# A chunked state-space stage whose front moves into the previous chunk's scan loop, with one more quarter of the summing on GpSimd for every second state

## The reference

```python
proj = einsum('blh,eh->ble', hidden, in_proj_w)
x, gate = proj[..., :1024], proj[..., 1024:]
u = silu(causal_conv4(x, conv_w) + conv_b)
dt_lr, Bm, Cm = split(einsum('bld,rd->blr', u, x_proj_w))       # 128 + 16 + 16
delta = softplus(einsum('blr,dr->bld', dt_lr, dt_proj_w) + dt_proj_b)
A = -exp(A_log)
h = h * exp(delta_t * A) + (delta_t * u_t) * B_t                 # 16 states for each of 1024 channels
y_t = sum over n of h[.., n] * C_t[n]
y = (y + u * D) * silu(gate)
out = einsum('bld,hd->blh', y, out_proj_w)
```

## Time and profile before

| | |
|---|---|
| median of 3 runs | 3812.79 us (3812.38 to 3813.08) |
| the profiled execution, its time | 3813.42 us |
| its span | 3811.6 us |
| PE, DVE, ACT, POOL busy in the span | 3318.6, 3286.4, 2489.4, 2454.7 us |
| mean granted TensorE clock | 0.942 |
| HBM traffic | 40 GB/s over the span |

### The profile page before, as it was taken

One profiled execution on the slowest core, in us unless ns is written; L12 is line 12 of the kernel. 1 busy time (PEld: TensorE's weight loads), 2 busy tenths in 40 slices (PEclk: granted clock), 3 DMA queues, 4 the chain that ended last, 5 costly groups with the idle time before them and its releaser, 6 DMA issues.

```text
span 3811.6 us, 46308 instructions
## 1 busy us (share of the span) xinstructions
PE 3318.6 (87%) x12672; PEld 2365.7 (62%) x12672; DVE 3286.4 (86%) x6128; ACT 2489.4 (65%) x4790; POOL 2454.7 (64%) x1943
## 2 busy tenths in 40 slices
PE   5888984999999999999999999999999999985738
PEld 4666662666767676767676767666666666663515
DVE  5888883299999998989898989898989898989891
ACT  4777672186767676767676858676767676765650
POOL 0344343086869595959595959595969595957470
PEclk8999997999999999999999999999999999987868
DMA  2222212111111111111111111111111111101010
GB/s 99 65 74 73 76 61 84 61 37 40 30 43 31 42 33 41 39 34 41 34 41 34 41 33 41 34 39 35 40 35 39 35 39 37 47 27 37 20 36 6
DMA packets 119378, 165.36 MB, mean 43 GB/s; under 512 B 8545, under 2 KB 84193, under 8 KB 118625
## 3 DMA queue, kind: packets, MB, share of 16 engines
q1 hardware_dynamic: 119136, 162.63, 15.2%
HBM read 128.39 MB, written 25.69 MB: 40 GB/s over the span
## 4 chain that ended last, share of the span: by engine, by line
POOL 28%; PE 20%; DVE 17%; issue 15%; ACT 2%; DVEq 1%; POOLq 0%; DMA 0%; SPq 0%; ACTq 0%
POOL dBu L866 16%; POOL yacc L879 12%; DVE D L1308 10%; PE W L1064 6%; PE W L1114 5%; PE W L1096 3%; PE W L1137 2%; DVE prod L1327 2%; PE W L1141 2%; DVE D L1330 2%; PE D L1064 1%; DVE U L1259 1%; DVE yacc L1339 1%; ACT L916 1%; DVE hT L1221 1%
## 5 line engine op out<-in xcount | busy, mean ns | idle before, releaser
L1308 DVE TENSOR_TENSOR_SCAN D<-D,hc,dBu 128x256 f32<-128x256 f32 x2048 | 1436.9, 740 | 47.0 <-ACT D L1007 47.0
L866 POOL TENSOR_TENSOR dBu<-U,BC 128x512 f32<-128x512 f32 x1024 | 1294.3, 1275 | 276.4 <-DMA BC<-bc_scratch 200.3
L1064 PE MATMUL W<-nT,wffn 128*128 128x256 f32 x5632 | 1241.6, 382 | 47.2 <-ACT nT L905 32.6
L1064 PEld LDWEIGHTS W<-nT,wffn 128*128 128x128 f32 x5632 | 1058.8, 189 | 230.6 <-ACT nT L905 37.5
L1007 ACT ACTIVATE D<-delta,A 128x256 f32<-128x256 f32 x2048 | 891.7, 468 | 425.7 <-DVE yacc L1339 404.8
L879 POOL TENSOR_TENSOR yacc<-yacc,prod 128x512 f32<-128x512 f32 x736 | 933.9, 1269 | 263.0 <-DVE prod L1327 258.5
L1096 PE MATMUL W<-wffn,hT 128*128 128x512 f32 (+1 forms) x1408 | 642.0, 613 | 41.5 <-DVE hT L1221 41.5
L1096 PEld LDWEIGHTS W<-wffn,hT 128*128 128x128 f32 (+1 forms) x1408 | 273.8, 197 | 373.4 <-issue 323.8
L1327 DVE TENSOR_TENSOR prod<-D,BC 128x512 f32<-128x512 f32 x736 | 494.6, 672 | 0.0
L1064 PE MATMUL W<-nT,win 128*128 128x256 f32 x2048 | 453.9, 383 | 33.7 <-ACT nT L905 33.7
L1064 PEld LDWEIGHTS W<-nT,win 128*128 128x128 f32 x2048 | 391.4, 192 | 106.4 <-ACT nT L905 44.9
(11 more groups left out here) (118 smaller groups left out, 3212.0 us busy)
## 6 DMA issues: line engine op xcount, KB each, us to landing
BC<-bc_scratch SPq DMA_DIRECT2D x256, 256.0 KB, 4.6
XM<-x_scratch SPq DMA_DIRECT2D x29, 512.0 KB, 4.9
X<-x_scratch SPq DMA_DIRECT2D x17, 512.0 KB, 3.6
ix<-idx SPq DMA_DIRECT2D x33, 255.0 KB, 2.9
X<-x SPq DMA_DIRECT2D x16, 512.0 KB, 3.4
XR<-x SPq DMA_DIRECT2D x16, 512.0 KB, 3.4
x_scratch<-XR SPq DMA_DIRECT2D x16, 512.0 KB, 3.7
out<-X SPq DMA_DIRECT2D x16, 512.0 KB, 2.8
```

The lines of the kernel that those rows point to most:

```text
L866: nc.gpsimd.tensor_tensor(dBu[e % 4][:], U[:, 2 * j:2 * j + 2, :], BC[slot][:, 0:1, :].to_broadcast([P, 2, CH]), ALU.mult).then_inc(s_dBu, 1)
L1064: last = T_.matmul(dst, lhsT, rhs, start=(n == 0), stop=(n == len(terms) - 1))
L1308: V.tensor_tensor_scan(D[:, m, :], D[:, m, :], dBu[e % 4][:, m % 2, :], hc[:, n, m:m + 1], ALU.mult, ALU.add).then_inc(s_scan, 1)
```

## The change

The front of chunk k = i + 1 is worked off within step i. Its first product stands on TensorE right behind the gate half of chunk i; its taps, convolution and Silu stand at fixed elements of loop i on ScalarE and VectorE; its low-rank and B/C products stand inside the late `ffn`, between the two downward products (`x_proj`), and its delta product (`delta_proj`) behind that `ffn`, one pair of D at a time as loop i gives it up. below, soft and to_delta of the pairs 0 to 2 run over the end of loop i, those of pair 3 over the end and the first element of loop i + 1. For this U * delta goes to a tile of its own (dU) and nT is double; the convolution reads W in PSUM directly (no xext), and the three columns at its edge are formed by GpSimd (`edges`) from a tile `tail` and added by VectorE (`ends`). The output projection stands undivided behind the first half of the gate product, its residual is added in two halves. XM keeps a chunk from the first gated layer to its norm for the state-space layer, so x2 isn't loaded back for that. The hand-placed table load (L960) is gone. The rescale of hc by keep becomes one memset at the start of the second sequence. Steps are written out for every chunk, with constants instead of registers. GpSimd's `add` takes pair 3 too where the state is even, in all chunks. `places` (the steady case is quoted) has all element numbers; the scratch for dynamic DMA is set to 4096.

```diff
+        def by_pool(e):
+
+            return e % 4 < 3 or e % 8 == 3
+
+        def upto(e):
+
+            return sum(by_pool(u) for u in range(e))
...
+                return dict(stat=stat, early=(1, 3), late=(8, 10), m=(NEVER, NEVER), m2=(41, 43), out=(4, 6),
+                            norm=5, gate=(9, 12), evac=18, silu=(21, 24, 27, 29, 32, 34), res=38,
+                            norm2=36, evac2=39, silu2=(44, 46, 49, 52, 54, 56), res2=NEVER, norm_m=NEVER, evac_m=NEVER, norm_m2=58, evac_m2=NEVER,
+                            taps=(14, 17), conv=(12, 14), smooth=(21, 21, 24, 24), low=61, bc=63)
...
+                def edges(k):
+
+                    pool.wait_ge(m_tail, 2 * k + 2)
+                    pool.wait_ge(m_edge, 2 * k)
+                    nc.gpsimd.tensor_tensor(edge[:], tail[:], cw[:, :, 0:1].to_broadcast([P, ME, KC - 1]), ALU.mult).then_inc(m_term, 1)
+                    for d in (1, 2):
+                        pool.wait_ge(m_term, 5 * k + 2 * d - 1)
+                        w = KC - 1 - d
+                        nc.gpsimd.tensor_tensor(term[:, :, 0:w], tail[:, :, d:KC - 1], cw[:, :, d:d + 1].to_broadcast([P, ME, w]),
+                                                ALU.mult).then_inc(m_term, 1)
+                        pool.wait_ge(m_term, 5 * k + 2 * d)
+                        nc.gpsimd.tensor_tensor(edge[:, :, 0:w], edge[:, :, 0:w], term[:, :, 0:w], ALU.add).then_inc(m_term, 1)
...
-                    N_.preload_act_table_set("natural_log_exp_and_others")
...
+                def taps(k, q):
+
+                    act.wait_ge(m_x, 2 * k + q // 2 + 1)
+                    act.wait_ge(m_du, 4 * k)
+                    for h in range(2):
+                        m = 2 * q + h
+                        N_.activation(U[:, m, :], W[q // 2][:, m % 4, :], ACT.Identity, bias=cb[:, m:m + 1],
+                                      scale=cw[:, m, KC - 1:KC]).then_inc(m_tap, 1)
+
+                def smooth(k, q):
+
+                    act.wait_ge(m_edge, 2 * k + q // 2 + 1)
+                    N_.activation(U[:, 2 * q:2 * q + 2, :], U[:, 2 * q:2 * q + 2, :], ACT.Silu).then_inc(m_u, 1)
...
+                def soft(k, j):
+
+                    act.wait_ge(m_below, 4 * k + j + 1)
+                    N_.activation(dBu[j][:], dBu[j][:], ACT.Exp).then_inc(m_exp, 1)
+                    act.wait_ge(m_exp, 4 * k + j + 1)
+                    N_.activation(dBu[j][:], dBu[j][:], ACT.Ln, bias=1.0).then_inc(m_ln, 1)
...
+                        if e == 0:
+                            soft(i, 3)
+                        if e < 4:
+                            skip(i, e)
+                        if f1 and e == at["norm"]:
+                            norm(norm_no(*early(i)), early_rows, ffn_no(*early(i)))
...
+                            if i + 1 < NC and e == at["taps"][h]:
+                                taps(i + 1, 2 * h)
+                                taps(i + 1, 2 * h + 1)
+                        if f1 and e == at["evac"]:
+                            evac(norm_no(*early(i)), i % 2, 0)
...
+                        if i + 1 < NC and e == at["low"]:
+                            low_rank(i + 1, 1 - side_late(i))
+                        if i + 1 < NC and e == at["bc"]:
+                            b_and_c(i + 1, 1 - side_late(i))
+                    if 0 < i < NC - 2:
+                        evac(norm_no("M", i + 2), i % 2, 0)
+                    for j in range(4):
+                        save(i, NE - 4 + j)
+                        if i + 1 < NC and j < 3:
+                            soft(i + 1, j)
...
+                def x_proj(k, side):
+
+                    pe.wait_ge(m_u, 4 * (k + 1))
+                    dt = chain(W[side][:, 0, :], [(wx[:, m, 0:R], U[:, m, :]) for m in range(ME)])
+                    dt.then_inc(m_dt, 1)
+                    bc = chain(W[side][0:2 * S, 2, :], [(wx[:, m, R:R + 2 * S], U[:, m, :]) for m in range(ME)])
+                    bc.then_inc(m_bc, 1)
+
+                def delta_proj(k):
+
+                    pe.wait_ge(m_dtl, k + 1)
+                    for j in range(4):
+                        if k:
+                            e = NE - 4 + j
+                            pe.wait_ge(s_prod, NE * (k - 1) + e + 1)
+                            pe.wait_ge(s_ha, pool_sums(k - 1) + upto(e + 1))
+                        for m in (2 * j, 2 * j + 1):
+                            last = T_.matmul(D[:, m, :], wdt[:, m * P:(m + 1) * P], dtl[:], start=True, stop=True)
+                        last.then_inc(m_dp, 1)
...
                     down(0, MI - 1)
+                    if low is not None:
+                        x_proj(low, 1 - side)
                     for k in range(MI):
                         if k == TURN_AT and then is not None:
+                            if low is not None:
+                                pe.wait_ge(m_bcS, low + 1)
                             turn(then, 1 - side)
                         last = down(1, k)
...
+                def step(i):
+
+                    done_norms = norm_no(*early(i)) if i + 2 < NC else norm_no(*late(i))
+                    done_ffns = ffn_no(*early(i)) if i + 2 < NC else ffn_no(*late(i))
+                    pe.wait_ge(n_T, done_norms)
+                    pe.wait_ge(f_res, done_ffns)
                     pe.wait_ge(m_bcS, i + 1)
-                    for h in range(2):
...
+                    for m in range(4):
+                        last = gate(i, m)
+                    last.then_inc(m_g, 1)
+                    if i:
+                        project(i - 1)
+                    for m in range(4, ME):
+                        if i and m % 2 == 0:
+                            pe.wait_ge(m_res, 2 * (i - 1) + m // 2 - 1)
+                        last = gate(i, m)
+                    last.then_inc(m_g, 1)
+                    L, F = norm_no(*late(i)), ffn_no(*late(i))
...
+                        first(i + 1, 0)
+                        pe.wait_ge(m_sg, 2 * i + 2)
+                        first(i + 1, 1)
+                        pe.wait_ge(m_tail, 2 * i + 5)
+                        free = (m_tail, 2 * i + 6)
...
+                def conv(k, q):
+
+                    dve.wait_ge(m_tap, ME * k + 2 * q + 2)
...
+                            if d:
+                                dve.wait_ge(m_conv, 24 * k + 6 * q + 2 * (d - 1) + h + 1)
+                            V.scalar_tensor_tensor(U[:, m, KC - 1 - d:CH], W[q // 2][:, m % 4, 0:CH - KC + 1 + d], cw[:, m, d:d + 1],
+                                                   U[:, m, KC - 1 - d:CH], ALU.mult, ALU.add).then_inc(m_conv, 1)
...
+                def ends(k, h):
+
+                    half = slice(4 * h, 4 * h + 4)
+                    dve.wait_ge(m_term, 5 * (k + 1))
+                    V.tensor_scalar(tail[:, half, :], W[h][:, :, CH - KC + 1:CH], keep[:, k + 1:k + 2], None, ALU.mult).then_inc(m_tail, 1)
+                    dve.wait_ge(m_conv, 24 * k + 12 * (h + 1))
+                    V.tensor_tensor(U[:, half, 0:KC - 1], U[:, half, 0:KC - 1], edge[:, half, :], ALU.add).then_inc(m_edge, 1)
+
+                def below(k, j):
+
+                    if k:
+                        dve.wait_ge(s_scan, 2 * NE * (k - 1) + 2 * (NE - 3 + j))
+                    dve.wait_ge(m_dp, 4 * k + j + 1)
+                    for h in range(2):
+                        m = 2 * j + h
+                        last = V.tensor_scalar(dBu[j][:, h, :], D[:, m, :], bdt[:, m:m + 1], CAP, ALU.add, ALU.min)
+                    last.then_inc(m_below, 1)
...
+                    for h in range(2):
+                        m = 2 * j + h
+                        step_ = V.scalar_tensor_tensor(delta[:, m, :], D[:, m, :], bdt[:, m:m + 1], dBu[j][:, h, :], ALU.add, ALU.max)
+                    step_.then_inc(m_delta, 1)
+                    dve.wait_ge(m_delta, 4 * k + j + 1)
+                    V.tensor_tensor(dU[:, pair, :], U[:, pair, :], delta[:, pair, :], ALU.mult).then_inc(m_du, 1)
...
+                            times_c(i, e - 1)
+                        if e == 1:
+                            to_delta(i, 3)
+                        if i and more and e >= NE - 2 and e <= NE:
+                            below(i + 1, e - NE + 2)
+                        if i and more and e >= NE:
+                            to_delta(i + 1, e - NE)
...
+                    gate_y(i)
+                    if at["res2"] > NE + 1:
+                        resid(ffn_no(*late(i)), late_rows, side_late(i))
+                    if i == 0:
+                        for j in range(3):
+                            below(1, j)
+                        to_delta(1, 0)
+                        to_delta(1, 1)
+                    if more:
+                        to_delta(i + 1, 2)
+                        below(i + 1, 3)
 
                 V.memset(hc[:], 0.0)
```

(48 more changed lines are left out.)

729 lines of the change are left out of this document (326 added, 403 removed).

## The result

The changed kernel takes 4181.9 us (median of 4 runs, 4181.4 to 4183.1) where the kernel before takes 3812.9 in the same comparison (3812.4 to 3814.5): ratio 1.0967, 95% interval 1.0948 to 1.0986. Slower, as forecast, by 369 us instead of 288, and 12 us above the range.

The account below looks back on a forecast made before the run. TensorE and VectorE were both busy 86 to 87%, neither the bound throughout; TensorE's waits in the new order were to decide. 3811.6 + 270 + 7 + 12 - 4 + 3 = 4100, adjusted to 4101 us; range 3960 to 4170.

Parts of the forecast that it names:

- TensorE's idle time before nT: Before the first product with nT in a steady chunk: TensorE idle some 15 us, evacuation placed behind the conv.
- the boundary: Passage from one chunk's step to the next: TensorE idle some 10 us at each.
- The eight loads of the forecast: ScalarE table loads at Exp and Ln changes: 8 a chunk, 2.8 us of them in the tail, 2.4 in the head.
- rival 1: Ln's table set also holds Exp: one load, 5.2 us less a chunk, 4024 us in total; chance 0.22.
- The share of GpSimd: Scan loop: 8 additions saved on VectorE (4.7 us), 8 extra on GpSimd (9.9), fitting in 127.5, cost and gain nothing.
- the steady period: Chunks 1 to 13: 58.6 + 127.5 + 20.8 = 206.9 us a chunk, 20.8 more than 186.1, +270 in all.
- chunk 0: First chunk: taps at 55 and 58, everything behind them in series, gate_y ahead of below: +12 us.
- the head: Steady chunk from its first scan until nT is evacuated: 0 to 58.6 us.
- TensorE's chain: Steady chunk from nT on, 58.6 to 186.1: products 125.1 us plus a cold start of 2.4, 127.5.
- the tail: End of a steady step, 186.1 to 206.9: below, softs, delta pairs, gate_y and residual, 20.8 us.
- Rival 4: ScalarE's places for Silu and the low-rank copy hold TensorE up inside the 127.5 too: over 4170 us; chance 0.04.
- Rival 3: TensorE lags so that nT waits for no one and the boundary is bridged: 176 a chunk, 3700 us; chance 0.04.

Follow-up runs that it names:

- e2: Changed kernel with ScalarE's evacuation of nT at element 15 instead of 18, ahead of the taps of the conv's second half: 4112.5 us.
- e4: Changed kernel with two of ScalarE's copies of the last hc columns (saves) placed before the first soft: 4090.1 us.
- e1: Changed kernel with the table set holding Exp and Ln loaded once ahead of the softs: 4102.7 us.
- e5: Changed kernel with GpSimd's share back to pairs 0 to 2 for every state, the pipeline alone: 4181.1 us.
- e7: Kernel before the change with only the new GpSimd share, pair 3 of every even state too: 3833.7 us.
- f2: Changed kernel with hand load, saves first, Silus kept together, earlier places, half of next gate product between delta pairs, and GpSimd's share back to pairs 0 to 2: 3850.4 us.
- g1: Changed kernel with the second delta pair of the next chunk moved behind gate_y and the residual: 4185.8 us.
- f3: Like f2 but with the new GpSimd share, the second delta pair moved as in g1 and the residual at element 63: 3802.1 us.
- g2: Changed kernel with only the places of chunk 0's second stage one to three elements earlier: 4186.5 us.
- f4: f3 with chunk 0's places earlier as in g2: 3807.8 us.

## Why the direction was right, and which terms failed

**The direction and the mechanism were right.** TensorE's idle time before nT (13.9, forecast some 15) and at the boundary is where the time goes; e2 and e4 took hold of one each and gained 69 and 92. The eight loads of the forecast are in the trace: 4 at Ln, 2 at the Exp of soft and 2 more than before at the loop's Exp; in all a steady chunk has 36 loads for 30. e1 is worth 79 where rival 1 stood 77 lower than the forecast. That the totals agree so well is partly luck: the steady chunks gave 61 for 68, the other parts 19 for 9. The Trainium skill's rule in "ScalarE: Activation LUTs", section "Table sets: the hidden batching unit", is true of the named set but did not come of itself: left to the automatic loads, each change between Ln and Exp brought a load. The 1.38 us of drain that the Trainium skill, "ScalarE: Activation LUTs", adds in its section "What ACT_TABLE_LOAD costs" doesn't show here either: in the rows of ScalarE above the Exp ends at 2452.41, the load runs from 2452.42 to 2453.70 and the Ln starts at 2453.72.

**The share of GpSimd costs nothing here** (e5: 1 us), as the prediction said; and it named its own condition, cover, without which e7 and f2 show 21 to 23 us, once for the worse and once for the better.

**The step that failed: terms of the sum were too small**, 288 us for 369, and most of it in two places: the steady period (57 of the 81 us) and chunk 0 (16).

1. *The steady period*, 206.9 forecast, 211.2 measured. In the chunk shown the head takes 60.9 for 58.6, TensorE's chain 127.5 for 127.5 and the tail 23.0 for 20.8 (on average over the chunks 61.2, 127.5 and 22.6).

In the tail the prediction took each pair of delta as if warm, at 0.9 us. The granted clock was 1.00 in the first group, which took 1.03, and 0.53, 0.50 and 0.50 in the three behind the waits, which took 1.96, 2.05 and 2.08; the prediction had charged the lower clock behind the long waits only. Two of these groups are on the path, 1 us each. gate_y took 3.42 for 2.4, since GpSimd works beside it in the new order (g1); the earlier trace rows had it where GpSimd was at rest. to_delta and the addition took 0.8 less than forecast.

In the head the scan of element 12 starts at 37.2 for 34.4. In between veps takes 1.33 us where the prediction took the 0.44 of the earlier trace rows for it, and nmr 1.22 behind a wait of 0.6 for the root, where it had 0.3 for the shifts. The traces show why. These tiny operations end with the operation that GpSimd has at work, to within 0.05 us:

```profile
2502.01 2.51 POOL L861 TENSOR_TENSOR dBu<-dU,BC 128x512 f32<-128x512 f32 x2
2503.22 1.33 DVE L1247 TENSOR_SCALAR veps<-mv 128x2 f32<-128x2 f32 x1
```

The kernel before has the same in the very chunk of the earlier trace rows, where veps stands twice more beside the 0.44: once behind GpSimd, and once in the front, with GpSimd at rest.

```profile
1635.88 1.27 POOL L866 TENSOR_TENSOR dBu<-U,BC 128x512 f32<-128x512 f32 x1
1636.09 1.08 DVE L1207 TENSOR_SCALAR veps<-mv 128x2 f32<-128x2 f32 x1
...
1682.91 0.17 DVE L1207 TENSOR_SCALAR veps<-mv 128x2 f32<-128x2 f32 x1
```

Of the 92 veps and nmr of its second stage 62 met a GpSimd operation and all 62 end so; the 30 that met none took 0.16 or 0.17. So the prediction read the price of a wait that happened to be short. Conv waits 1.22 for its taps, which stand behind the gate's Silu and its two table loads on ScalarE, where the prediction had 1.6 for GpSimd's outer product: another wait of about the same size.

Two slips are in the sums. The cold start was taken at 2.4, but 16.53 (the 64 matmuls at 736.49 in the kernel before) less 13.98 is 2.55 (here the 176 matmuls behind the wait took 40.77 for 38.15, 2.6). The terms of the tail up to below(2) add up to 9.6, not 10; they measured 12.4.

2. *Chunk 0*, +28.4 for +12, 16 us. TensorE's waits there sum to 15.99 + 4.46 + 0.25 + 15.06 + 6.58 = 42.3 us up to x_proj, and to 5.00 + 0.20 + 2.55 + 1.39 + 5.24 = 14.4 in the kernel before, a difference of 28. The prediction counted the serial end (taps, conv, Silu, low) but not the 16.0 us for which TensorE waits for the chunk's first norm, where the kernel before has no wait. In e1, which differs only by the loads by hand, they are 6.7 (6.5 in f3), and the first scan stands 6.4 us earlier; chunk 0 itself still takes 207.6 for 210.6, and 205.7 in e4. So the loads (3.0) and the order of the softs (4.9) hold some 8 of its 28 us.

```profile
803.18 1.94 PE L1079 MATMUL W<-ident,nrm 128*128 128x128 f32 x8 [15.99 <-ACT nrm L926]
...
956.34 1.97 PE L1079 MATMUL W<-ident,nrm 128*128 128x128 f32 x8 [15.06 <-DVE tail L1301]
964.88 9.72 PE L1071 MATMUL W<-U,wx 128*128 128x256 f32 x32 [6.58 <-ACT U L941]
```

Moving the places did not help there (g2, f4). What holds the other 20 us stays open.

**Rival 4** gave the right side of the range for a reason that was not the one at work: inside the 127.5 us TensorE waits 0.8 in all, and what lifted the time was the head, the tail and chunk 0. **Rival 3** (176 a chunk) did not occur, and f3, which comes nearest to it, shows what it takes: the named set, saves first, Silus that share loads, the evacuation ahead of the second conv half, the gate product between the pairs. With all of it the period is 184.3 against 186.1, 2 of the some 11 us that the earlier trace rows left; in the chunk shown TensorE still has six waits of 1.0 to 2.7 us, 10.2 together.

## What to carry to other kernels

Before two stages are overlapped, add up the waits of the engine whose work can't shrink, in the new order: here the front had been cheap because its operations stood in one block, with one table load, a warm TensorE and GpSimd at rest. Spread through a loop, each piece pays the load, the lower clock and the shared access anew, and a queue in program order turns one late input into a wait for all behind it (the nT evacuation behind the conv's taps: 13.9 us a chunk). If you price a tiny operation of VectorE from one row, look at several: beside GpSimd veps took 0.44, 1.08 and, in the changed kernel, 1.33 us. If you move an operation of ScalarE, look at whose table load it shared.

## What the runs showed of the hardware

- VectorE's product of two SBUF operands and GpSimd's lengthen one another: VectorE's took 2.36, 2.93 and 3.42 us at 0, 0.7 and 2.2 us of overlap. GpSimd's took 2.18 us for 1.27 where it started 0.16 us behind VectorE's, and 1.27 where it started 0.55 us ahead of it. The product of D, which lies in PSUM, with BC takes 0.67 beside GpSimd and 0.68 without. The Trainium skill, "GPSIMD Engine Reference", section "Specifications", lists such contention for VectorE instructions with two SBUF inputs; these rows agree.
- The 128x2 operations veps and nmr, 0.16 to 0.17 us with GpSimd at rest, end together with the GpSimd operation that they meet (62 of 62 in the kernel before) and so take 0.43 to 1.22 us there, up to 1.35 in the steady chunks of the changed kernel. The norm statistics of 128x512 beside them are not lengthened: two take 1.27 us beside GpSimd and 1.28 with it at rest. This is read from the times of the rows, not from a run that changed it.
- After 3.8 us of waiting four matmuls took 1.96 and 2.05 us, at a granted clock of 0.53 and 0.50; after 2.5 us of waiting the first such group took 1.10 at 1.00, and the next, after another 2.5, 2.04 at 0.50 (e1).
- Automatic table loads change sets between Exp and Ln in turn; by hand one set serves both (e1: no load between them).
